# A gated recurrence with attention on one core: VectorE's two recurrences written out without a loop, TensorE's counts kept in registers, logits stored first

## The reference

```
# 1: GRU, keys x[t] (512 x 64)
z = sigmoid(x@Wx_z + h@Wh_z + b);  r = sigmoid(x@Wx_r + h@Wh_r + b)
hh = relu(x@Wx_h + b_in + r * (h@Wh_h + b_rec))
h  = z*h + (1 - z)*hh                       # outs[t] = h
logit[b, t] = sum_u outs[t, b, u] * (queries @ W_att.T)[b, u]
a = softmax(logit, axis=time)
# 2: attention GRU over outs[t], weight a[t] per sequence
r = sigmoid(outs@Wx_r + h@Wh_r + b);  c = relu(outs@Wx_c + b + r * (h@Wh_c))
h = (1 - a[t])*h + a[t]*c                    # the result is the last h
```

## Time and profile before

| | us |
|---|---|
| median of 3 runs (4427.02 to 4429.88) | 4429.84 |
| the profiled execution | 4430.53 |
| its span | 4428.7 |
| VectorE busy | 4196.2 |
| ScalarE busy | 2286.8 |
| GpSimd busy | 2717.1 |
| first recurrence, first to last gated of group a | 16.23 to 2315.13 |
| second recurrence, the same | 2352.69 to 4424.15 |

### The profile page before, as it was taken

How to read it: one execution, slowest core, us unless ns; L and a number is a source line. 1 busy time by engine, 2 the same in 40 slices (tenths; PEclk the granted TensorE clock), 3 DMA queues, 4 the chain that set the end, 5 groups by cost and what they waited for, 6 DMA issues and landing times.

```text
span 4428.7 us, 336421 instructions
## 1 busy us (share of the span) xinstructions
PE 4372.4 (99%) x131196; PEld 3968.0 (90%) x131196; DVE 4196.2 (95%) x24625; ACT 2286.8 (52%) x9363; POOL 2717.1 (61%) x6154
## 2 busy tenths in 40 slices
PE   8999999999999999999998999999999999999999
PEld 7888888888888888888887999999999999999998
DVE  8999999999999999999998999999999999999999
ACT  5666666666666666666654444444444444444444
POOL 6777777777777777777773444444444444444444
PEclk9999999999999999999998999999999999999999
DMA  3333333333333333334334555555555555554554
GB/s 110 115 116 123 115 116 123 115 115 121 117 115 120 119 115 120 119 115 121 118 123 129 129 132 128 128 132 128 128 133 128 128 133 128 128 133 129 127 133 115
DMA packets 169275, 544.13 MB, mean 123 GB/s; under 512 B 31644, under 2 KB 38060, under 8 KB 169260
## 3 DMA queue, kind: packets, MB, share of 16 engines
q1 hardware_dynamic: 169260, 543.93, 44.3%
HBM read 405.24 MB, written 138.56 MB: 123 GB/s over the span
## 4 chain that ended last, share of the span: by engine, by line
DVE 52%; PE 21%; issue 20%; DMA 3%; DVEq 2%; SPq 1%; ACT 0%; ACTq 0%; PEldq 0%
DVE vec_bank L525 12%; DVE gated L448 8%; DVE state L538 7%; DVE a_new L532 6%; DVE vec_bank L455 5%; DVE gated L519 5%; DVE vec_bank L464 5%; DVE h L475 4%; PE r_bank_a L561 4%; PE r_bank_b L561 3%; DMA logits<-logit_rows 2%; PE logit_bank L623 2%; PE z_bank_b L569 2%; PE z_bank_a L569 2%; PE c_bank_a L561 1%
## 5 line engine op out<-in xcount | busy, mean ns | idle before, releaser
L331 POOL TENSOR_TENSOR a_kept<-attn_rest,state 128x128 f32<-128x128 f32 x2048 | 933.6, 456 | 1173.6 <-DVE state L538 1139.0
L314 POOL TENSOR_TENSOR kept<-z_gate,h 128x128 f32<-128x128 f32 x2048 | 933.6, 456 | 533.8 <-ACT z_gate L360 512.0
L304 POOL TENSOR_TENSOR prod<-h,qw 128x128 f32<-128x128 f32 x2050 | 934.6, 456 | 0.0
L569 PE MATMUL r_bank_a<-x,weights 64*64 64x128 f32 x8200 | 881.7, 290 | 12.8 <-ACT r_gate L389 7.1
L569 PE MATMUL r_bank_b<-x,weights 64*64 64x128 f32 x8192 | 892.8, 295 | 0.0
L569 PE MATMUL z_bank_a<-x,weights 64*64 64x128 f32 x8200 | 853.9, 283 | 0.0
L569 PE MATMUL z_bank_b<-x,weights 64*64 64x128 f32 x8192 | 843.3, 283 | 0.0
L623 PE MATMUL logit_bank<-prod,row_sum 64*64 64x128 f32 x8208 | 798.5, 270 | 8.6 <-ACT logit_rows L349 5.0
L464 DVE SCALAR_TENSOR_TENSOR vec_bank<-vec_bank,z_rest 128x64 f32<-128x64 f32 x4096 | 735.9, 225 | 0.4 <-issue 0.3
L475 DVE TENSOR_TENSOR h<-vec_bank,kept 128x64 f32<-128x64 f32 x4096 | 721.3, 218 | 0.0
L389 ACT ACTIVATE r_gate<-r_bank_a 128x128 f32<-128x128 f32 x1024 | 284.0, 277 | 837.5 <-PE r_bank_a L561 837.5
(11 more groups left out here) (119 smaller groups left out, 17857.4 us busy)
## 6 DMA issues: line engine op xcount, KB each, us to landing
x<-in_keys_t SPq DMA_DIRECT2D x512, 256.0 KB, 3.7
gru_outputs<-h SPq DMA_DIRECT2D x256, 512.0 KB, 2.9
x<-gru_outputs SPq DMA_DIRECT2D x512, 256.0 KB, 3.7
attn<-attention SPq DMA_DIRECT2D x512, 256.0 KB, 3.9
logits<-logit_rows SPq DMA_DIRECT2D x258, 8.0 KB
time_rows<-logits SPq DMA_DIRECT2D x2, 896.0 KB, 7.0
attention<-time_rows SPq DMA_DIRECT2D x2, 896.0 KB, 5.5
weights<-in_weight_columns SPq DMA_DIRECT2D x2, 176.0 KB, 3.7
```

What stands on the lines that cost most here:

```text
L304: nc.gpsimd.tensor_tensor(prod[:, (s - 1) % BODY, gcols(g)], h_at(s - 1)[:, gcols(g)], qw[:, gcols(g)], ALU.mult).then_inc(prod_ready[g], 1)
L314: nc.gpsimd.tensor_tensor(kept[:, g], z_gate[:, g], h_at(s - 1)[:, gcols(g)], ALU.mult).then_inc(kept_ready[g], 1)
L331: nc.gpsimd.tensor_tensor(a_kept[:, s % 2, gcols(g)], attn_rest[:, s % 2, gcols(g)], state[:, (s - 1) % 2, gcols(g)], ALU.mult).then_inc(a ...
L569: last = nc.tensor.matmul(dst[lanes(half)], weights[lanes(1 - half), w], moving[lanes(1 - half)], start=start, stop=False, skip_group_chec ...
```

## The change

1. **VectorE.** Both loops are gone; the 1024 steps of each recurrence are written out. Waits compare with constants. `bodies_begun` and the two waits at s == 0 are gone. The register adds, branches and reloads of its loops go with them.
2. **Sigmoid semaphores.** `r_ready` and `ar_ready` are split into one for even and one for odd steps, and TensorE sets each back by HALF = 4.
3. **TensorE's counts.** They stay in registers from body to body and are added to once where used, instead of being computed from `t0` in each body.
4. **TensorE's second loop.** Its pass now ends after the matmuls on a_new of group a for the next step (`agru_state(0, ...)`); before, it ended ahead of them.
5. **SP.** The logits' store stands between the first x load of a pass and the outputs' store.

```diff
 SP, first loop
                     load_x(keys, k + 1, b)
+                    if b == 0:
+                        store_logits(k)
                     store_outs(k, b)
-                store_logits(k)
 ScalarE
-  nc.scalar.activation(r_gate[:, g], r_bank[g][:, 0:GC], ACT.Sigmoid).then_inc(r_ready[g], 1)
+  nc.scalar.activation(r_gate[:, g], r_bank[g][:, 0:GC], ACT.Sigmoid).then_inc(r_ready[g][s % 2], 1)
 VectorE, first recurrence
+            def by_parity(s):
+                return s % BODY // 2 + 1
             def gru_gated(due, s, g):
-                if s == 0:
-                    dve.wait_ge(r_summed[g], due)
-                    dve.sem_inc(bodies_begun, 1)
                 dve.wait_ge(rh_summed[g], due)
-                dve.wait_ge(r_ready[g], s + 2)
+                dve.wait_ge(r_ready[g][s % 2], by_parity(s))
...
-            with dve.Fori(0, T, BODY) as t0:
-                stored = t0 * ONES + 16
-                for s in range(BODY):
-                    due = t0 + (s + 2)
-                    for g in GROUPS:
-                        gru_gated(due, s, g)
-                        gru_cand(due, s, g)
-                        gru_new(due, s, g)
-                        gru_h(due, stored, s, g)
+            for s in range(T):
+                for g in GROUPS:
+                    gru_gated(s + 2, s, g)
+                    gru_cand(s + 2, s, g)
+                    gru_new(s + 2, s, g)
+                    gru_h(s + 2, 16 * (s // BODY + 1), s, g)
 VectorE, second recurrence
             def agru_gated(due, s, g):
-                if s == 0:
-                    dve.wait_ge(ar_summed[g], due)
-                    dve.sem_inc(bodies_begun, 1)
-                dve.wait_ge(ar_ready[g], s + 2)
+                dve.wait_ge(ar_ready[g][s % 2], by_parity(s))
                 dve.wait_ge(rc_summed[g], due)
...
-            with dve.Fori(0, T, BODY) as t0:
-                pairs = t0 * PAIRS + 32
-                done = t0 + 1
-                for s in range(BODY):
-                    due = t0 + (s + 2)
+            for s in range(T):
+                loaded = 32 * (s // BODY + 1)
...
 TensorE, first loop
-            with pe.Fori(0, T, BODY) as t0:
-                full, loads = count(0, t0, BODY), [count(1, t0 * PAIRS, 32), count(2, t0 * PAIRS, 64)]
+            copied, loads = counts[:2]
+            pe.reg_mov(copied, BODY)
+            pe.reg_mov(loads, 32)
+            with pe.Fori(0, T, BODY):
...
-                        pe.wait_ge(r_ready[o], seen_by_pe(s, o))
+                        pe.wait_ge(r_ready[o][(n - 1) % 2], by_parity(n - 1))
...
+                        if g == 1 and n == CHUNK:
+                            pe.reg_add(loads, loads, 32)
...
+                        if s == 2 and g == 0:
+                            pe.reg_add(copied, copied, BODY)
 TensorE, second loop
-            with pe.Fori(0, T, BODY) as t0:
-                soon = count(0, t0, 1)
...
+            agru_state(0, 0, 0)
+            with pe.Fori(0, T, BODY):
                 for s in range(BODY):
-                    due, soon = soon, count((s + 1) % 2, t0, s + 2)
...
+                    agru_ahead(0, s, s)
+                    pe.reg_add(count[(s + 1) % 2], count[s % 2], 1)
+                    agru_state(1, s, s + 1)
+                    agru_ahead(1, s, s + 1)
+                    agru_state(0, (s + 1) % BODY, s + 1 if s < BODY - 1 else 0)
```

More of the change, by code:

```diff
@@ L29, in recurrent_attention_kernel @@
     ROW0 = BODY
-    PAIRS, ONES = 32 // BODY, 16 // BODY
+    PAIRS = 32 // BODY
     outs_dram = nc.dram_tensor("gru_outputs", (BODIES, 2, P, CHUNK, COLS), F32).ap()
@@ L56, in part_sems, with parity_sems @@
             return [[sem(f"{name}_{'ab'[g]}{part}") for part, _ in PARTS] for g in GROUPS]
+        def parity_sems(name):
+            return [[sem(f"{name}_{'ab'[g]}_{('even', 'odd')[parity]}") for parity in range(2)] for g in GROUPS]
         weights = sb("weights", [P, 11, U])
@@ L338, in _ @@
                 act.sem_inc(zr_ready[g], FIRST)
-                for q in (r_ready[g], ar_ready[g]):
-                    act.sem_inc(q, (1, FIRST)[g])
+            act.sem_inc(r_ready[1][1], HALF)
+            act.sem_inc(ar_ready[1][1], HALF)
             act.sem_inc(rest_ready, 1)
@@ L460, in gru_new @@
                 for part, c in PARTS:
-                    dve.wait_ge(cand_ready[g][part], (due, s + 2)[part])
+                    dve.wait_ge(cand_ready[g][part], (due, s % BODY + 2)[part])
                     if part == 0:
-                        dve.wait_ge(zr_ready[g], s + 2)
+                        dve.wait_ge(zr_ready[g], s % BODY + 2)
                     nc.vector.scalar_tensor_tensor(new[:, c], cand[:, c], 0.0, z_rest[:, g, c],
@@ L586, in _ @@
             counts = [pe.alloc_register(f"pe_count_{i}") for i in range(4)]
-            def count(i, base, more):
-                pe.reg_add(counts[i], base, more)
-                return counts[i]
             pe.wait_ge(w_loaded, 16 * N_WEIGHT_DMAS)
@@ new lines, in _, with agru_state @@
+            count, loads = counts[:2], counts[2:]
+            def agru_state(g, s, n):
+                ns = a_new[:, (s - 1) % 2, gcols(g)]
+                o = 1 - g
+                pe.wait_ge(anew_ready[g][(s - 1) % 2], ANEW[s - 1])
+                own(r_bank[g][:, 0:GC], AH_R, ns, False, True).then_inc(ar_summed[g], 1)
+                pe.wait_ge(ar_ready[o][(n - 1) % 2], by_parity(n - 1))
+                if g == 1 and n % CHUNK == 0:
+                    b = n // CHUNK % 2
+                    pe.wait_ge(x_loaded[b], loads[b])
+                    pe.reg_add(loads[b], loads[b], 32)
+                agru_x_r(o, n, (acand_ready[g], -BODY) if s == 0 else None)
+                own(hid_part(g), AH_C, ns, False, True).then_inc(rc_summed[g], 1)
@@ new lines, in agru_ahead @@
+            def agru_ahead(g, s, n):
+                o = 1 - g
+                alone()
+                pe.wait_ge(agated_ready[o], count[n % 2])
+                pe.wait_ge(akept_ready[o], count[n % 2])
+                last = own(hid_part(o), AH_C, from_kept(o, n), True, False)
+                seen = (n - 2) % BODY
+                if seen in (BODY - 2, BODY - 1):
+                    last.then_inc(anew_ready[o][seen % 2], -HALF)
+                pe.wait_ge(axr_summed[o], n + 1)
+                last = own(r_bank[o][:, 0:GC], AH_R, from_kept(o, n), False, False)
+                if (n - 1) % BODY >= BODY - 2:
+                    last.then_inc(ar_ready[o][(n - 1) % 2], -HALF)
+                pe.wait_ge(acand_ready[o], seen_by_pe(s, o))
+                agru_x_c(o, n, (x_used, CHUNK) if g == 0 and s % CHUNK == CHUNK - 1 else None,
+                         (axr_summed[o], -BODY) if s == BODY - 1 else None)
@@ new lines, in _ @@
+            pe.reg_mov(count[0], 1)
+            pe.reg_mov(loads[1], 32 * (BODIES + 1))
+            pe.reg_mov(loads[0], 32 * (BODIES + 3))
+            agru_state(0, 0, 0)
+            with pe.Fori(0, T, BODY):
+                for s in range(BODY):
+                    agru_ahead(0, s, s)
[3 more added lines that the diff above has]
+                    agru_state(0, (s + 1) % BODY, s + 1 if s < BODY - 1 else 0)
```

87 lines of the change are left out of this document (31 added, 56 removed).

## The result

| | us | ratio to before, 95% interval |
|---|---|---|
| before, median of 4 runs (4426.97 to 4429.88) | 4428.43 | |
| after, median of 4 runs (4227.70 to 4228.54) | 4227.98 | 0.9548 [0.9531, 0.9564] |
| forecast | 4187 (4150 to 4262) | |

The kernel became 200 us faster. The direction held and the time lies in the range, 41 us above the forecast.

A forecast was written before the change was run, and what follows sets the result against it. VectorE's own sequence, busy 95% of the span, was taken as the bound. From 4430.5 us, 110 and 138 for the two recurrences' loops came off and 5 for code was added: 4187 us, range 4150 to 4262.

The forecast's parts named there:

- terms 1 and 2: VectorE's loops written out: first recurrence 2298.90 to 2189.2 us, gain 110; second 2071.46 to 1933.4, gain 138.
- Rival 1: Partner engines bind: steps stay at 2.16 us in the first recurrence, 1.92 in the second; 4250 us, chance 0.17.
- rival 3: The turns don't go: TensorE's own turn keeps 0.5 us a body in the first loop; 4251 us, chance 0.06.
- term 3: TensorE's turns: second loop's moved end 0 to 22 us, 10 left as cost; register adds nothing, at most 10.
- term 5: Fetching VectorE's written-out code: 210 packets at 0.23 us, a cost of 0 to 48 us, 5 taken.
- rival 2: VectorE's straight-line code isn't prefetched, each packet is waited for, 2.3 us each; 4665 us, chance 0.08.
- term 4: Logits stored first removes ScalarE's 39.0 us store wait; already in the first recurrence's gain, by itself 0 to 39.
- term 1: VectorE's first recurrence loop: step 2.14 us without register adds and turns, 2189.2 against 2298.90 us, a gain of 110.

The follow-up runs named there:

- joined: Kernel after, x-load add moved, axc_summed wait dropped, candidate matmul and sigmoid counting up one semaphore so gated waits once, both recurrences: 4204.9 us.
- more code: Kernel after plus three increments of an unused semaphore per half step in VectorE's first recurrence, 6144 instructions in all: 4262.7 us.

## Why the prediction was right, and where it was off

**The turns (terms 1 and 2): right.** No step is long by its place in the body any more, except by TensorE's add. The first recurrence's plain step is 2.129 us, forecast 2.14; the second's 1.873, forecast 1.88. That is 11 and 7 us better, the 11 about what the rounding of the rows allowed. In the second recurrence gated starts 0.04 behind the sigmoid, as forecast (3003.21 + 0.28 = 3003.49, gated at 3003.54; 0.042 as the median of plain steps):

```profile
3003.21 0.28 ACT L397 ACTIVATE r_gate<-r_bank_a 128x128 f32<-128x128 f32 x1 [0.65 <-PE r_bank_a L554]
3003.33 0.29 DVE L529 SCALAR_TENSOR_TENSOR a_new<-vec_bank,attn 128x128 f32<-128x128 f32 x1
```

Yet the sigmoid is hardly what sets the step. Gated also starts 0.21 behind a_new (3003.33), and group b's gated keeps that same distance in the kernel before, where its sigmoid had been done for 0.09 us:

```profile
3004.13 0.28 ACT L389 ACTIVATE r_gate<-r_bank_b 128x128 f32<-128x128 f32 x1 [0.38 <-PE r_bank_b L561]
3004.29 0.29 DVE L532 SCALAR_TENSOR_TENSOR a_new<-vec_bank,attn 128x128 f32<-128x128 f32 x1
3004.50 0.28 DVE L519 TENSOR_TENSOR gated<-c_bank_b,r_gate 128x128 f32<-128x128 f32 x1
```

So it is VectorE's own pace, which I had put at 1.86 as the lower bound, and the sigmoid comes just in time for it. Rival 1, steps at 2.16 and 1.92, didn't occur, nor rival 3.

**TensorE's turns (term 3): nothing, where I left 10 us.** The place of the end hides it; the value that it would have had, 16.3 us, lies within my 0 to 22.

**TensorE's register adds (term 3): mis-sized.** I costed them at nothing, with 10 us as the bound, "beside queued matmuls". The two a body in the second loop stood between the matmuls that gated waits for: 0.07 us x 256 = 18 us, of which moving one line gave 15.5 back. The bound failed because it took VectorE's 0.02 us an add as the price, not the place. That the first loop's turn "also loses the recomputed counts", which I had left at nothing, was worth something with VectorE's loops gone (2.21 against 2.13 us in one step of eight); how much with the logits stored first, no run shows.

**Code (term 5): the term that failed most.** I took 5 us of 0 to 48. The crossings cost 173 x (2.304 - 2.129) = 30.3 us in the first recurrence, and in the second 112 x (2.071 - 1.873) = 22.2, 52.5 in all, just above the bound. (Some 2 of the 22 belong to the adds, since some crossings fall into their steps.) Two steps of the working were wrong. The first was the queue and the count: I read TensorE's q8 (4 packets) and divided by its instructions, 176 a packet, which gave 210 packets. VectorE's own row stands beside it, for the first body of the kernel before:

```profile
q14 instruction: 3, 0.02, 0.4%
```

Too few packets and too high a price nearly cancel: 285 crossings at 0.18 stand for 210 packets at 0.23, so the 48 was close. What failed was the second step, to take 5 on the ground that VectorE asks more seldom; no row gave the 5. The kernel before has what is most likely the same stall in that same body of VectorE's timeline: a pair of operations that takes 0.36 elsewhere takes 0.56, and the next starts 0.20 late.

```profile
28.48 0.36 DVE L464 SCALAR_TENSOR_TENSOR vec_bank<-vec_bank,z_rest 128x64 f32<-128x64 f32 x2
...
30.63 0.56 DVE L464 SCALAR_TENSOR_TENSOR vec_bank<-vec_bank,z_rest 128x64 f32<-128x64 f32 x2
31.10 0.35 DVE L475 TENSOR_TENSOR h<-vec_bank,kept 128x64 f32<-128x64 f32 x2
```

At 0.20 us, 288 packets would have been 58 us. The Trainium skill, "Runtime: NRT & Kernel Launch", section Instruction fetch mechanics, says that passing into the next block, of 256 instructions, is mostly hidden. Here it isn't: the packets hold 128 instructions, and 285 crossings cost 0.18 us each. The trace agrees in that code is fetched ahead: 31 of the first recurrence's 173 crossings cost nothing, and rival 2's 2.3 us a packet is far off.

**The logits' store (term 4): right result for a poor reason.** I wrote that the 39.0 us of wait were "already in term 1" and by themselves between 0 and 39. On the kernel before the edit is worth 9 us. But with VectorE's turn gone it is worth 117, and without it the first recurrence would have been longer than before. The forecast was right because the edit was there; had I forecast VectorE's part alone, term 1's 110 us would have been off by 136 (2325.5 against 2189.2).

**The sum.** Against 2189.2 and 1933.4, with 5 for code, stand 2209.0 and 1957.9:

| | first | second |
|---|---|---|
| plain steps, 1023 x (measured - forecast) | -11 | -7 |
| crossings | +30 | +22 |
| TensorE's turn | 0 | -10 |
| TensorE's adds | 0 | +18 |
| not assigned | +1 | +1 |
| sum | +20 | +24 |

44 less the 5 that I had for code is 39, near the 41 us that the median lies above the forecast. That the time lies in the range is in part luck: code and adds together came 65 us above their values, both outside their own bounds, and 28 us of it were made up by shorter steps and by a turn that cost nothing.

## What to carry to other kernels

When a loop's turn is removed, look for what it covered: a wait that was short or absent behind a turn (here for a store, ahead of a sigmoid on the same engine) may get the turn's time back as a deficit, so an edit's worth on the kernel before can be a tenth of its worth on the one after (9 and 117 us here). Written-out code on a saturated engine had its price by the instruction here, and a second wait on an operation was an instruction: look for the price in the first pass of the old loop, on that engine's own instruction queue. An operation priced at 0.02 us cost 0.07 where it stood ahead of a matmul that the next engine waits for, and next to nothing a few lines further down.

## What the runs showed of the hardware that was not expected

VectorE's instructions come in packets of 8 KB, 128 to a packet, and a crossing isn't a fixed price. In the first recurrence it costs 0.12 us where 157 fall into 2198 us (joined), 0.18 where 173 fall into 2209 (after), and 0.30 where 220 fall into 2245 (more code); in the second some 0.1 with 80 (joined), 0.18 with 96 and 0.20 with 112 in some 1950. The more instructions a step has, the more a crossing cost here. It goes by the place in the step, too. In the kernel after, a crossing at group a's gated cost 0.00 us each time, one at its candidate 0.20 and one at group b's gated 0.30, each within 0.03 us over some 16 crossings; with more code none was free (0.20 to 0.34). Why a place is free or dear is open. So an instruction that does nothing has a price: 34.7 us for 6144, 5.6 ns each, 11.3 us for the 2048 that went in the first recurrence, and 6.2 for those in the second. The packets follow the count of VectorE's instructions: 37,193 in 294, 35,145 in 278, 33,097 in 262, 31,049 in 246. Steps without a crossing were 2.128 or 2.129 us in all these kernels.
